# Another head for the first batch of an attention and low-rank FFN kernel

## The reference

```python
xn = (x - mean(x)) / sqrt(var(x) + 1e-5)             # over the 256 features
q, k, v = xn @ wq.T + bq, xn @ wk.T + bk, xn @ wv.T + bv
attn = softmax(q @ k.T / 16) @ v                     # per batch
w = W + up_aux @ (lora_up @ (lora_down @ down_aux))  # 256 x 256
out = x + attn + xn @ w.T + b
```

## Time and profile before

| what | value |
|---|---|
| time, median of 3 runs | 516.13 us (515.81 to 516.21) |
| profiled execution | 516.27 us |
| its span, first to last instruction | 514.5 us |
| TensorE busy | 503.9 us, 98% |
| VectorE, ScalarE, GpSimd busy | 71%, 54%, 72% |
| first instruction of TensorE | 6.62 us |

### The profile page before, as it was taken

The page is one execution under the profiler, slowest core; times in us unless marked ns, Lnnn a source line. Parts: engine busy times, 40 slices in busy tenths (PEclk is TensorE's granted clock), DMA queues, the critical chain, the costliest instruction groups (busy, mean ns, idle before and its releaser), DMA issues.

```text
span 514.5 us, 8100 instructions
## 1 busy us (share of the span) xinstructions
PE 503.9 (98%) x2948; PEld 446.3 (87%) x2948; DVE 367.5 (71%) x839; ACT 276.6 (54%) x589; POOL 372.9 (72%) x221
## 2 busy tenths in 40 slices
PE   4999999999999999999999999999999999999997
PEld 4777897989989898898989989898998989889897
DVE  4789876876679585895858767686757758476594
ACT  2755677265754747367382665736474462725450
POOL 2843795986879966999669978699688976671730
PEclk9999999999999999999999999999999999999999
DMA  8020005000050002200050100501003010000002
GB/s 241 38 83 0 1 4 203 1 41 2 1 204 1 41 1 85 121 2 41 1 189 17 43 2 0 205 1 42 0 22 103 1 42 1 41 1 2 41 1 82
DMA packets 8694, 25.04 MB, mean 49 GB/s; under 512 B 1850, under 2 KB 3792, under 8 KB 7760
## 3 DMA queue, kind: packets, MB, share of 16 engines
q1 hardware_dynamic: 7328, 24.38, 13.1%
q10 hardware_dynamic: 1328, 0.16, 0.2%
HBM read 16.15 MB, written 8.39 MB: 48 GB/s over the span
## 4 chain that ended last, share of the span: by engine, by line
PE 96%; DMA 1%; ACT 1%; DVE 1%; issue 0%; ACTq 0%; DVEq 0%
PE o_ps L1080 12%; PE o_ps L1079 11%; PE o_ps L1078 11%; PE g_ps L998 10%; PE g_ps L999 10%; PE g_ps L1000 10%; PE s_ps L998 9%; PE s_ps L999 8%; PE s_ps L1000 8%; DMA bk_col<-in_L_attn_bk 1%; PE o_ps L998 1%; PE g_ps L1020 1%; PE o_ps L1000 1%; PE o_ps L999 1%; ACT prod L607 1%
## 5 line engine op out<-in xcount | busy, mean ns | idle before, releaser
L507 POOL TENSOR_TENSOR p_lo<-s,p_hi 128x1024 fp32r<-128x1024 f32 x60 | 143.8, 2429 | 38.8 <-ACT p_hi L657 38.8
L650 ACT ACTIVATE s<-s,e 128x512 f32<-128x512 f32 x128 | 84.3, 714 | 116.2 <-DVE s L848 116.1
L1080 PE MATMUL o_ps<-v_lo,p_hi 128*128 128x256 f32 x480 | 136.1, 283 | 0.0
L1079 PE MATMUL o_ps<-v_hi,p_lo 128*128 128x258 f32 x480 | 135.1, 282 | 0.0
L1078 PE MATMUL o_ps<-v_hi,p_hi 128*128 128x258 f32 x480 | 134.6, 281 | 0.0
L1078 PEld LDWEIGHTS o_ps<-v_hi,p_hi 128*128 128x128 f32 x480 | 91.3, 190 | 1.7
L1079 PEld LDWEIGHTS o_ps<-v_hi,p_lo 128*128 128x128 f32 x480 | 91.1, 190 | 1.6
L1080 PEld LDWEIGHTS o_ps<-v_lo,p_hi 128*128 128x128 f32 x480 | 90.2, 188 | 0.0
L807 DVE SCALAR_TENSOR_TENSOR tile_max<-s_ps,e,tile_max 128x512 f32<-128x512 f32 x80 | 59.9, 749 | 32.7 <-PE s_ps L1000 30.6
L998 PE MATMUL s_ps<-xt_hi,zt_hi 128*128 128x512 f32 x192 | 74.9, 390 | 0.0
L999 PE MATMUL s_ps<-xt_lo,zt_hi 128*128 128x512 f32 x192 | 74.7, 389 | 0.0
(11 more groups left out here) (157 smaller groups left out, 989.2 us busy)
## 6 DMA issues: line engine op xcount, KB each, us to landing
out<-base SPq DMA_DIRECT2D x15, 512.0 KB, 2.7
x_sb<-in_L_attn_x SPq DMA_DIRECT2D x7, 1024.0 KB, 8.2
x_t<-in_x_t SPq DMA_DIRECT2D x6, 1024.0 KB, 6.0
x_sb<-in_L_attn_x SPq DMA_DIRECT2D x4, 256.0 KB, 6.5
out<-base SPq DMA_DIRECT2D x4, 128.0 KB, 1.9
s<-in_L_attn_wk SPq DMA_DIRECT2D x1, 256.0 KB, 3.0
s<-in_L_attn_wq SPq DMA_DIRECT2D x1, 256.0 KB, 5.7
s<-in_L_attn_wv SPq DMA_DIRECT2D x1, 256.0 KB, 7.1
```

The costliest lines, as they stand in the source:

```text
L507: nc.gpsimd.tensor_tensor(p_pair(g, p_lo_sb, j), s_pair(j), p_pair(g, p_hi_sb, j).bitcast(f32), ALU.subtract).then_inc(p_lo_made, 1)
L650: nc.scalar.activation(s[:, n, :], s[:, n, :], ACT.Exp, bias=e[b % 2][:, n:n + 1]).then_inc(p_made, 1)
L1079: nc.tensor.matmul(o[:, 0:D + ONES], lo, v_hi[i][:, n, 0:D + ONES], start=False, stop=False)
L1080: mm = nc.tensor.matmul(o[:, 0:D], hi, v_lo[i][:, n, :], start=False, stop=last)
```

## The change

Order of loads: the first two tiles of x ahead of wk, then two more tiles, wq, wv, the rest of x and the FFN weight. The two small biases and the two LoRA factors come in one array (`small_in`, 128 partitions by 58) that the host lays out, by one DMA on ScalarE's queue; down_aux and up_aux go to SyncE's queue.

The first batch goes by pairs of tiles: statistics and deviation in stages of 2, 2 and 4 tiles, normalisation of even tiles by ScalarE and odd ones by VectorE, transposes of a pair in one bank (`turn`). V and FFN of a pair are separate groups of 256 columns per tile: `first_v` for three pairs ahead of or between z and the scores, `first_ffn` and the last `first_v` behind the scores. ScalarE copies an FFN pair to `base[1]`, GpSimd adds it to `base[0]`. A is made in plain float32 in two halves, around the second pair's transposes, so wk and wq are not split. Ahead of all that TensorE transposes the identity 24 times. z's biases stand ahead of the first transposes.

GpSimd's products of e_row and xn for batch 1 move to the head, batch 1's bias sum goes ahead of the shift of chunk 1, and batch 2's statistics move from the head on VectorE to the end of chunk 0. `make_stat_cols(2)` and `make_stat_row(2, ...)` move to later places in chunk 1. Other batches keep their order.

```diff
 (SyncE)
+            load_first(0)
+            sp.dma_start(wk_sb, rows(wk)).then_inc(wk_loaded, DMA)
+            load_first(1)
+            sp.dma_start(wq_sb, rows(wq)).then_inc(wq_loaded, DMA)
+            sp.dma_start(wv_t_sb, rows(wv_t)).then_inc(wv_loaded, DMA)
+            load_first(2)
+            load_first(3)
+            sp.dma_start(ffn_t_sb, rows(ffn_w_t)).then_inc(ffn_loaded, DMA)
...
 (GpSimd)
+            def add_first_ffn(j):
+                pool.wait_ge(first_ffn_copied, j + 1)
+                tiles = slice(2 * j, 2 * j + 2)
+                nc.gpsimd.tensor_tensor(base[0][:, tiles, :], base[1][:, tiles, :], base[0][:, tiles, :], ALU.add)\
+                  .then_inc(first_ffn_added, 1)
...
+            for j in range(PAIRS):
+                make_first_prod(1, j)
+            pool.wait_ge(x_bias_made, 1)
+            for j in range(PAIRS - 1):
+                add_first_ffn(j)
             shift_raw(0)
+            make_p_lo(0)
+            add_first_ffn(PAIRS - 1)
+            pool.wait_ge(first_ffn_added, PAIRS)
+            make_x_bias(1)
+            shift_raw(1)
+            make_rstd(2)
+            make_p_lo(1)
             for b in range(B):
...
                 if b + 2 < B:
                     norm_x_t(b + 2, 0)
                 shift_raw(CHUNKS * (b + 1))
...
 (ScalarE)
+            make_xn(0)
+            act.wait_ge(wv_loaded, DMA)
+            nc.scalar.activation(vf_hi[:, :, 0:D], wv_t_sb, ACT.Copy).then_inc(wv_hi_made, 1)
+            turned_hi(0)
+            make_xn(2)
+            turned_hi(1)
             act.wait_ge(a_mm, 1)
...
+            for n in range(TILES):
+                make_second_xn(n)
+            act.wait_ge(bias_made, 1)
+            for j in range(PAIRS):
+                copy_first_ffn(j)
             make_p(0, 0)
             make_p(0, 1)
             make_p_hi(0, 0)
+            first_v_hi(3)
...
-                if c == 0 and b + 2 < B:
+                if c == (0 if b else 1) and b + 2 < B:
                     make_stat_cols(b + 2)
...
 (VectorE, in the loop over chunks g, b = g // 2, c = g % 2)
-                if b + 2 < B and c == 1:
+                if 0 < b < B - 2 and c == 1:
                     make_stat_row(b + 2, 0)
                 make_tile_max(g + 1, 0)
                 make_tile_max(g + 1, 1)
-                if b + 2 < B and c == 1:
+                if 0 < b < B - 2 and c == 1:
                     make_stat_row(b + 2, 1)
...
                 make_groups_lo(b, c, 1)
                 if g == 0:
                     make_out(b, c * QT + 1)
+                if g == 1:
+                    make_stat_row(2, 0)
+                    make_stat_row(2, 1)
...
                 make_groups_lo(b, c, 2)
+                if g == 0:
+                    nc.vector.tensor_reduce(e_row_sum[:, :], e_row, AXIS, ALU.add).then_inc(e_row_sum_made, 1)
+                    dve.wait_ge(x_loaded[0], DMA)
+                    make_stats(2, range(TILES))
+                    make_mean_var(2)
...
 (TensorE; WARM = 24)
+            pe.wait_ge(identity_made, 1)
+            for _ in range(WARM):
+                nc.tensor.transpose(s_ps[2][:, 0:PT], identity[:, :], identity[:, :])
+
             pe.wait_ge(bq_spread, DT)
             pe.wait_ge(wk_loaded, DMA)
...
             mm.then_inc(b_parts_mm, 1)
+            turn(0)
+            make_a(0)
+            turn(1)
+            make_a(1).then_inc(a_mm, 1)
+            first_v(0)
+            first_v(1)
...
+            first_z(0)
...
+            first_z(1)
+            turn(2)
+            turn(3)
             pe.wait_ge(b_parts_made, 1)
...
+            scores(0, 0)
+            first_v(2)
+            scores(0, 1)
+            first_z(2)
+            first_z(3)
+            for n in range(2, TILES):
                 scores(0, n)
...
+            for j in range(PAIRS):
+                first_ffn(j)
+            first_v(3)
```

More of the change, by code:

```diff
@@ L274, in two, with pair, group_bank, rstd_count @@
             return ap.rearrange("p (t n) -> p t n", t=DT)
[L276 to L283, removed]
-            return g_ps[k % 2]
[L286 to L296, removed]
+        def pair(ap):
+            return ap.rearrange("p (m n) -> p m n", m=2)
+        TURN_BANKS = (g_ps[0], g_ps[1], g_ps[1], s_ps[3])
+        FIRST_V_BANKS = (o_ps[0], g_ps[0], o_ps[0], o_ps[0])
+        FIRST_Z_BANKS = (s_ps[0], s_ps[1], o_ps[0], o_ps[1])
+        FIRST_FFN_BANKS = (o_ps[0], o_ps[1], o_ps[0], o_ps[1])
+        RANK_BANK = s_ps[3]
+        WARM = 24
+        def group_bank(k):
+            return g_ps[k % 2]
+        def rstd_count(b):
+            return len(STAGES) + b
+        def stage_of(tile):
+            return [first <= tile < end for first, end in STAGES].index(True)
+        def prods(b):
+            return PAIRS * (b + 1)
+        def pair_of_columns(j):
+            return slice(2 * j * PT, (2 * j + 2) * PT)
         LAST = CHUNKS * B - 1
@@ L348, in _, with load_first @@
         def _(sp):
-            sp.dma_start(wk_sb, rows(wk)).then_inc(wk_loaded, DMA)
-            for j in range(4):
+            def load_first(j):
                 n = TILES // 4
@@ L567, in _ @@
         def _(act):
[L568 to L583, removed]
+            act.dma_start(small[:, :], small_in).then_inc(small_loaded, DMA)
@@ new lines, in first_v_hi, with make_z_hi, first_z_hi @@
+            def first_v_hi(j):
+                act.wait_ge(first_v_mm, j + 1)
+                nc.scalar.activation(v_hi[0][:, 2 * j:2 * j + 2, 0:D], pair(FIRST_V_BANKS[j][:, :]), ACT.Copy)\
+                  .then_inc(first_v_hi_made, 1)
+            def make_z_hi(ps, h, d):
+                return nc.scalar.activation(zt_hi[:, d, half(h)], ps[:, :], ACT.Identity, bias=z_bias[:, d:d + 1])
+            def first_z_hi(k):
+                act.wait_ge(first_z_mm, k + 1)
+                make_z_hi(FIRST_Z_BANKS[k], *HALVES[k]).then_inc(first_z_hi_made, 1)
@@ L1001, in split_products, with turn @@
                 return mm
+            def turn(j):
+                pe.wait_ge(xn_made, j + 1)
+                pe.wait_ge(first_xn_made, j + 1)
+                if j == 2:
+                    pe.wait_ge(turned_lo_made, 2)
+                elif j == 3:
+                    pe.wait_ge(mid_rank_made, 1)
+                for d in range(DT):
+                    for m in range(2):
+                        mm = nc.tensor.transpose(TURN_BANKS[j][:, (2 * d + m) * PT:(2 * d + m + 1) * PT],
+                                                 xn[:, 2 * j + m, d * PT:(d + 1) * PT], identity[:, :])
+                mm.then_inc(turned_mm, 1)
@@ L1005, in group @@
                 i = b % 2
[L1006 to L1011 removed]
+                wait(pe, group_done, groups(b, k) - 2)
+                if shifts:
+                    pe.wait_ge(shifted, shifts + k % 2)
                 if k < NT:
                     h, d = HALVES[k]
[L1014 to L1018 removed]
+                    if d == 0:
+                        pe.wait_ge(xn_made, PAIRS + (h + 1) * TILES // 2)
```

472 lines of the change are left out of this document (256 added, 216 removed).

## The result

The changed kernel takes 522.71 us, median of 4 executions (521.79 to 523.23), against 516.07 for the kernel before: ratio 1.0127 with a 95% interval of 1.011 to 1.0145. It is slower by 6.6 us. The forecast was 521.1 us with a range of 517.0 to 525.5. The profiled execution took 521.79 us, its span is 519.7.

What follows compares the result with a forecast made beforehand. The prediction took TensorE, busy 98% of the span, as the bound. It summed 516.27 - 5.0 (head) + 0.9 (FFN copies) - 0.5 (old wait) + 9.4 (late rows) = 521.1 us, range 517.0 to 525.5.

Steps and rivals of the forecast that it cites:

- the head: Start up to chunk 1's first score: new order brings that landmark from 48.17 to 43.2 us, gain 5.0.
- the late rows: Batch 2's row statistics, later on VectorE, start GpSimd's first normalisation 12.65 us later; TensorE loses 9.4 us in chunk 2's product.
- the 0.5 that went: TensorE's wait on VectorE at 86.96 us disappears because the rows leave the head of VectorE's list; 0.5 us won.
- The faster rival: GpSimd's first normalisation starts before 99.7 us, so the stage loses under 4.0 us and the head wins; chance 0.11.
- The wait on the V groups: TensorE waits some 4 us near 107 us, as ScalarE stands still for normalised halves; same delay, not more.
- The wait on p's low parts: In chunk 2's product with V, TensorE waits three times, 1.7 us each, between 124 and 131 us.
- VectorE's lateness: In the head, VectorE must finish its list up to the third V pair first, 0.8 us late.
- ScalarE's FFN copies: At chunk 1's start, they delay chunk 0's exponentials, so the eighth score waits for the second raw copy; 0.9 us lost.
- Full pace after the 24 transposes: In the head, TensorE was taken to run at full pace from 6.7 us, after the identity's transposes.
- the half-pace rival: Warming transposes don't raise the pace, which doubles only after A: gain 1.1, total 525.0 us; chance 0.13.
- The pace lost in new waits: Rival: TensorE loses its pace in the late rows' waits, adding half of a 5 us bound, 523.6 us; chance 0.10.
- Late wv: Rival in the head: second pair waits for wv landing at 10.8 us, VectorE's list late; gain 3, 523.1 us; chance 0.08.

Runs made afterwards that it cites:

- Experiment 1: Changed kernel with batch 2's statistics, deviation, columns and rows back in their old places, new head kept; 513.62 us, ratio 0.9957.
- experiment 3: Kernel before, with only batch 2's two row instructions moved to their later place; 524.96 us, ratio 1.0184.
- experiment 2: Changed kernel with batch 2's two rows one place earlier, behind chunk 2's second shift, ahead of the third V pair; 519.11 us, ratio 1.0067.
- experiment 5: Changed kernel with 32 identity transposes put into TensorE's 3.9 us wait on the V groups; 524.06 us, ratio 1.0157.
- experiment 4: Changed kernel without the 24 warming transposes of the identity; 525.11 us, ratio 1.0179.
- experiment 6: Kernel before plus 24 identity transposes ahead of its first product; 516.25 us, ratio 1.0008.
- experiment 8: Changed kernel, batch 2's statistics and columns early, rows behind chunk 2's second and fourth maxima, second x pair scaled before deferrable work; 511.60 us, ratio 0.9919.

## Why the prediction was right

The forecast's form held: the head gains, the late rows lose more, and nothing gives it back. That the total came so near is in part luck, since the errors of its terms cancel.

- **The late rows, 9.4 us forecast.** Right in place, releaser and nearly in size: 11.84 us of idle time ahead of the first normalisation, released by VectorE's transposition, and about 9.1 us lost (8.9 in the stretch, less 0.3 for the raw copy, plus the 0.5 that went). Experiment 1 takes it away, 3 gives it to the old kernel alone, and 2 scales it one to one with GpSimd's gap. The faster rival needed a start before 99.7 us of the old count; it began at 101.66, which with the 3.8 us of the head is 105.5 of the old count, where 105.7 was forecast (the working wrote 102.92 + 0.4 as 103.25 on the way, 0.07 too little). The wait on the V groups is part of the same delay, as forecast: experiment 5 fills it, and the fourth part stays where it was behind the landmark.
- **The wait on p's low parts** was forecast as three of 1.7 us. It was two, 2.1 in all. Part of the difference is the first clock fall, by which TensorE arrived 2.4 us later: in experiment 5, without that fall, the waits were three, 3.3 in all.
- **The head, 5.0 forecast, 3.8 measured** between the two profiled executions, and 2.5 where the first small load lands at the same time. That is the term furthest off. A was done at 12.25 where 12.15 was said. This hides misses that cancel. The first tile of x landed at 4.6, not 3.75, and its statistics began at 5.27, behind VectorE's copy, which the sum doesn't have. wv landed at 7.8, not 9.0. The last step of the sum, ScalarE's scaling of the third tile, took 0.59 us where 0.55 was said and was not what the second pair waited for: that was VectorE's scaling of the fourth tile, which the sum leaves out. It began at 9.61 and took 1.35 us beside GpSimd's product. (The working's 10.85 is 10.80 by its own terms.) Against the 3.8, the missing 1.2 us lie behind A, where the trace lists no wait: from A to the last two z it took 13.96 instead of 13.1 us, and from there to the landmark 18.2 instead of 18.0. Each small group up to the last z cost 0.1 to 0.3 more than its products at the steady spacing (a z of six products 1.59 and 1.50 instead of 1.36, the delta 1.06 instead of 0.85). In all that is 1.65 us; the forecast had only 0.8 there, booked as VectorE's lateness, which doesn't appear as a wait. The mis-sized terms are these dozen groups, priced by their spacing alone; why a change of group costs more, no run shows. The other 1.3 us, down to 2.5, are the first load's landing: the forecast's base of 48.17 is an execution with the load at 6.21.
- **ScalarE's FFN copies, 0.9 forecast**: the wait on the raw copy is 0.3. The bound from below was nearer.
- **The clock.** Full pace after the 24 transposes was right in the profiled execution, and experiment 4 shows what it is worth; in experiment 2 it came later. That experiment 4, at 525.1, lands beside the half-pace rival's 525.0 is by another sum: a landmark 2.1 us later, and a second fall. The pace lost in new waits (523.6) came true in its event and not in its price in the profiled execution: the fall at 107.8 is hidden behind GpSimd. Experiments 2, 4 and 5 show a second fall, at the product with V, that is not hidden and costs 1.5 to 1.8 us (389.5 becomes 391.0 to 391.3 to the end). The executions of the changed kernel at 523.2 may have it; they have no trace, so this stays open.
- **Late wv**: refuted, 7.8 us.

The sum came out 0.7 us below the profiled execution: the head 1.2 too good, and 0.4 behind the fourth part and around the span that it did not have, against 0.6 too much loss for the raw copy and 0.3 for the late rows. The median is another 0.9 above that execution; where this lies, no trace shows.

## What to carry to other kernels

When work is moved to a later place on an engine with slack, look for whoever reads its result in order: VectorE had 30% free, but GpSimd's list stood still for 11.84 us behind two transpositions of 2.4. On an engine busy for 94% of a stage a delay of its head passes to the end less only its idle time, so the late item's place in both lists counts and not its cost. Try the halves of a change apart: here one was worth -2 us and the other +9, and keeping the first without the second gave the best kernel. And compare a landmark over several executions: here it moved by 0.8 us with the landing of the first loads.

## What the runs showed of the hardware

- Transposes of the identity alone brought TensorE to full pace in the changed kernel (at 5.37 us, begun at 1.52); in experiments 2 and 6 the 24 ran at half pace to their end, 5.38 us. In experiment 6 the granted clock fell to 0.50 at the end of a wait of 1.5 us.
- Pacing by another engine can lower the clock too. In experiment 2 TensorE waited twice on GpSimd, 2.6 us in all, and then ran its packed part at half clock:

```profile
127.10:130.40 3.30, 3.30 (x17) 3.30 (x16) 3.04 (x6) 0.60 (x1) 3.30 (x3) 0.50 0.00 0
```

  In the changed kernel and in experiment 3 it waited there 2.1 us in all, and the clock stayed at 1.00.
- A float32 scaling of VectorE from SBUF took 0.41 us in experiment 8 and 1.35 in the changed kernel beside GpSimd's product of two tensors, where it ended at 10.96, just behind the product's end at 10.81; that product took 1.71 us instead of the next one's 1.27. The Trainium skill, "Advanced Engine Details and Errata", GPSIMD Details, says that GpSimd shares a read and a write interface with VectorE; both durations agree with that.
